# A spiking delta-rule attention block with routed experts: the first right-hand side formed ahead of the decay step, a later decay step put behind the first tile

## The reference, cut to what matters

```python
mem = DECAY * mem + sdt
hard = (mem > THR)                      # spike
mem = mem - spike * THR
alpha = sigmoid(abt + alpha_spike * spike)
beta  = sigmoid(bbt + sum(spike * beta_spike))
alpha = where(any hard, alpha, 1); beta = beta * any hard
s = s * alpha
u = einsum(kt, s)
s = s - beta * outer(kt, u) + beta * outer(kt, vt)
out = einsum(s, qt)
```

## Time and profile before

| | |
|---|---|
| three runs, us | 2068.42, 2074.34, 2077.52 (median 2074.34) |
| profiled execution, us (its span; the page shows nothing around it) | 2078.1 |
| mean granted TensorE clock in it | 0.858 |
| busy: TensorE, VectorE, ScalarE, GpSimd | 70%, 62%, 29%, 17% |
| chunks 0 to 6, end of the solve | 224.2, 428.5, 647.6, 865.3, 1076.7, 1288.8, 1503.7 |
| chunks 0 to 6, start of w0 | 230.7, 440.1, 657.5, 875.1, 1085.1, 1300.3, 1513.5 |
| chunks 0 to 6, start of w1 | 239.5, 448.9, 666.2, 883.9, 1093.9, 1309.1, 1522.2 |

### The profile page before, as it was taken

The page is one execution under the profiler, slowest core; times in us unless marked ns, Lnnn a source line. Parts: engine busy times, 40 slices in busy tenths (PEclk is TensorE's granted clock), DMA queues, the critical chain, the costliest instruction groups (busy, mean ns, idle before and its releaser), DMA issues. The chain is left out here.

```text
span 2078.1 us, 46460 instructions
## 1 busy us (share of the span) xinstructions
PE 1457.7 (70%) x18280; PEld 903.1 (43%) x18280; DVE 1279.4 (62%) x3385; ACT 596.6 (29%) x1212; POOL 348.5 (17%) x505
## 2 busy tenths in 40 slices
PE   1246886788778877797779776977797779566551
PEld 0113463256334643464336433653365336345541
DVE  1737766865577647865786478557965675343335
ACT  1132124322521243123413341324223412212221
POOL 2120031003200140014101410140013101100005
PEclk9577998899779988999799879987998789769995
DMA  2161000000010001000100010001000100302112
GB/s 72 72 253 22 19 10 7 21 19 21 2 26 19 10 13 27 16 12 13 27 16 12 12 27 16 12 13 27 11 17 12 23 16 12 103 17 76 33 30 81
DMA packets 110570, 64.74 MB, mean 31 GB/s; under 512 B 79873, under 2 KB 91329, under 8 KB 110354
## 3 DMA queue, kind: packets, MB, share of 16 engines
q1 hardware_dynamic: 99186, 38.52, 7.1%
q10 hardware_dynamic: 8448, 16.78, 2.2%
q0 software_dynamic: 2720, 6.36, 1.0%
HBM read 27.39 MB, written 34.24 MB: 30 GB/s over the span
## 5 line engine op out<-in xcount | busy, mean ns | idle before, releaser
L775 POOL COPY kx<-kend_t 32x256 f32<-32x256 f32 x256 | 113.1, 442 | 859.6 <-PE ps L1274 843.3
L1655 DVE SCALAR_TENSOR_TENSOR state<-state,gam,ps 128x128 f32<-128x128 f32 x512 | 137.5, 341 | 74.3 <-PE ps L1274 74.3
L1211 PE MATMUL ps<-wv,ident 128*128 128x512 f32 x320 | 169.1, 661 | 9.2 <-DVEq L1590 9.2
L1607 DVE TENSOR_TENSOR nv<-ps,nrm 128x512 f32<-128x512 f32 x64 | 44.2, 691 | 182.1 <-PE ps L1146 181.6
L1467 DVE TENSOR_TENSOR kq_leaf<-kq,eleaf 128x1024 f32<-128x1024 f32 x32 | 39.7, 1239 | 161.4 <-ACT dleaf L892 114.5
L1274 PE MATMUL ps<-w,kx 128*64 128x128 f32 x2048 | 132.5, 285 | 0.0
L1579 DVE TENSOR_TENSOR tmp<-kq,kq_blk 128x31 f32<-128x31 f32 (+15 forms) x248 | 115.2, 464 | 12.7 <-ACT mem L827 6.7
L1274 PEld LDWEIGHTS ps<-w,kx 128*64 128x64 f32 x2048 | 116.9, 143 | 13.6 <-issue 13.6
L1069 PE MATMUL ps<-yt,headind 128*16 128x512 f32 x128 | 87.1, 819 | 38.6 <-ACT yt L865 28.6
L1211 PEld LDWEIGHTS ps<-wv,ident 128*128 128x128 f32 x320 | 64.9, 213 | 90.4 <-issue 74.5
L1107 PE MATMUL ps<-kq_pair 64*32 64x32 f32 x2048 | 60.3, 220 | 61.5 <-DVE ab L1514 56.5
(11 more groups left out here) (317 smaller groups left out, 3188.3 us busy)
## 6 DMA issues: line engine op xcount, KB each, us to landing
slot_d<-zeros ACTq DMA_DIRECT2D x16, 1024.0 KB, 13.1
a_d<-kq_pair SPq DMA_DIRECT2D x8, 512.0 KB, 2.6
kq_blk<-a_d SPq DMA_DIRECT2D x32, 128.0 KB, 3.6
u_d<-kq SPq DMA_DIRECT2D x8, 512.0 KB, 2.6
ub<-u_d SPq DMA_DIRECT2D x128, 32.0 KB, 2.0
wall<-in_w SPq DMA_DIRECT2D x8, 512.0 KB, 8.0
xin<-slot_d SPq DMA_DIRECT2D x39, 64.0 KB, 1.8
made_d<-ye SPq DMA_DIRECT2D x39, 64.0 KB, 1.5
```

Source lines behind the costliest of these rows:

```text
L775: m = pool.tensor_copy(kx[part, :, b4, :], kend_t[part, g, 2 * q:2 * q + 2, :])
L1211: pe.matmul(bw.t[:, :], ident[:, :], wv[:, 0:512], start=True, stop=True)
L1655: k = dve.scalar_tensor_tensor(out=state[:, hp, b, :], in0=state[:, hp, b, :], scalar=gam[:, hp, b:b + 1], in1=bd[j].t[:, DV * x:DV * x + ...
```

## The change

VectorE's instructions are put in another order: `aff` and step 0 stand behind r0 and ahead of nv1, no longer ahead of r0. TensorE's step 1 (ab2 alone) stands at the end of tile 0, behind d0, no longer between v1 and w0. TensorE's other steps, and all of ScalarE's, GpSimd's and SyncE's instructions, stay where they are.

```diff
@@ TensorE, body @@
                     if i + 1 < TILES:
                         values(c, i + 1)
-                    if nxt and i + 1 < STEPS:
+                    if nxt and 0 < i < STEPS - 1:
                         decays(nxt, i + 1)
...
                         if b4 >= 2:
                             m.then_inc(bd[b4 % 2].full.sem, 1)
+                    if nxt and i == 0:
+                        decays(nxt, 1)
@@ VectorE, body @@
             solve(c, nxt, last)
             values(c, 0)
-            if last:
-                head_on_vector(dve, last, room, "aff")
-            if nxt:
-                decays(nxt, 0)
             for i in range(TILES + 1):
...
                     dve.tensor_tensor(r[:, :, :], nv[:, :, :], bp.t[:, :].rearrange("p (h v) -> p h v", v=DV),
                                       ALU.subtract).then_inc(bp.drained.sem, 1)
+                    if i == 0:
+                        if last:
+                            head_on_vector(dve, last, room, "aff")
+                        if nxt:
+                            decays(nxt, 0)
                     if i + 1 < TILES:
                         values(c, i + 1)
```

## The result

The changed kernel takes 2084.8 us (median of 20 runs), the kernel before 2072.1 us (20 runs beside them): ratio 1.0063, 95% interval 1.0041 to 1.0086, that is +13 us (+8.5 to +17.8). A later series on another chip gave 1.0065 (1.0028 to 1.0103). The forecast was 2081 and +6.6 us: right in direction and inside its range, too small by half, and on the other side of the 0.5% that the text had set as no change.

A forecast was written before the change was run, and what follows sets the result against it. No engine fills the span; a chain of handovers bounds the kernel. 11.2 us lost behind d0 less 4.6 gained in front gives +6.6 us, added to the 2074.34 median: 2081 us, 0.3% slower, range 2066 to 2091.

The forecast's parts named there:

- ab2 behind d0: Tile 1: r1 hangs on alpha2, which needs ab2, so w1 starts 1.6 us later; 11.2 us over seven chunks.
- w2: After w1: 1.3 us of slack is left before w2, so nothing more is late.
- r0 in the front: Before w0: r0 delays ab1, v1, w0 by 0.61 us in five chunks, 3.05 us; hidden in chunks 1 and 5.
- The low clock: Chunks 3 and 6: w0 moves into the 1.2 GHz stretch, taking back 0.6 us each, 1.2 us.
- the gain: Solve to w0 over seven chunks: 8.86 from ab2 leaving, less 3.05 for r0 and 1.2 for the clock, 4.6 us.
- The rival's: Before ab1: longer TensorE idling makes the clock fall more often, 1.34 us per low stretch; 2088 us, slower; chance 0.24.
- three signs of being wrong: w0 ahead of ab1; w0 to w1 below 9.7 us; or 1.2 GHz stretches in fronts that had none.
- w0 released by r0: Front: early r0 lets w0 start once `ub` has landed, as in chunk 7; 2064 us, faster; chance 0.08.
- The covered wait: Behind d0: r1 comes in time and r0 costs nothing, ab2 only changes place; 2071.5 us, no change; chance 0.10.

The follow-up runs named there:

- the filler: The changed kernel plus one filler product (two passes of 512 columns) on TensorE between ab0 and ab1; 1.0062 of the kernel before.
- TensorE's half alone: The kernel before with only the change's TensorE hunks, ab2 behind d0, VectorE's order as before; 1.0092 of the kernel before, +19 us.
- the second one: Profile of the unaltered changed kernel run once more beside two others on one chip; 1.0065 of the kernel before, profiled execution 2076.4 us.
- e5_spread: Against the changed kernel: only ab0 in front, ab1 and cnt0 behind p1, ab2 behind y0, r1 ahead of alpha1; 1.0114 of the kernel before, +24 us.
- v1 first: The changed kernel with ab2 behind p1 and v1 moved on TensorE between ab0 and ab1; 0.9939 and 0.9992 of the kernel before in two series.
- e2_vector_only: The kernel before with only the change's VectorE hunks, TensorE as before; 1.0006 of the kernel before, +1 us.

## Why the prediction was right, and where it fell short

- **ab2 behind d0** (forecast w1 1.6 us later, 7 x 1.6 = 11.2): right. At full clock w0 to w1 is 10.36 against 8.77, and with the filler, which keeps the clock up from w0 to w1, the seven chunks give 11.2 us. r1 behind alpha2 ends the wait, as forecast, and moving ab2 ahead in tile 0 takes 0.6 us of it away in each chunk; the other 1.0 is ab2's own room. The forecast had cnt1 ahead of r1's end and costing nothing; so it is, but by 0.36 us only, and r1 ahead of alpha2 gives back no more than that.
- **w2** (forecast "nothing more is late"): nearly. w1 to w2 is 7.90 against 7.82, 0.6 us over seven chunks.
- **r0 in the front** (0.61 us in five chunks, hidden in two): right by mechanism. In chunk 4 of the changed kernel alpha0 waits 2.51 us and r0 is free; with TensorE's half alone, w0 waits for r0. That r0 had to move for ab2's move to be worth anything was only half seen: the 0.24 us between r0 and w0 was in the rows.
- **The low clock** is the term that was mis-sized. I let it take 0.6 us in two chunks. In the changed kernel's profiles every front whose ab1 waits 1.6 us or more has a low stretch behind it that reaches w0 or ends just at it: four of seven, and six of seven in the second one. The other profiles bear this out. In the thirteen that have ab1 in front (all but e5_spread's), the granted clock fell between the start of that wait and w0 in 30 of the 31 fronts where ab1 waited 1.6 us or more, in 5 of the 6 where it waited 1.20 to 1.45 us, and in none of the 54 where it waited 1.12 us or less. The one of the 31 that kept its clock is chunk 0 of before (1.78 us). From w0 to w1 the low clock takes 75.36 - 72.41 = 2.95 us (2.0 in the second), and up to w0 the gain was 3.03 us, not 4.6 (3.65 in the second). Together with w2: 11.19 + 0.56 + 2.95 - 3.03 = 11.7, against the forecast 6.6 and the measured 13. So the forecast's mechanism carried the sign. The rival's, to which I gave 0.24 and the time 2088, carried 2.95 of the 5.1 us that were missing in this stretch, and the shorter gain up to w0 another 1.6. Of the prediction's three signs of being wrong one came true: chunks 0 and 4, at full clock from the solve to w1 before, have a low stretch in both profiles.

  By kind of front, from the solve to w1: where the clock is low ahead of ab0, 20.3 us became 20.7 (+0.4; forecast 1.6 - 1.15); where it is low behind ab1, 18.55 became 19.9 (+1.3; forecast 1.6 - 0.5); at full clock 17.2 became 18.2, seen only with the filler. None of the 14 fronts in the changed kernel's two profiles is at full clock from the solve to w1, as chunk 4 was before; that shift of kinds is part of the 11.7. It also makes the 3.03 us up to w0 partly luck: chunk 1 gained 2.57 us (forecast 1.15), as its fillers now ran at full clock, and chunks 4 and 6 lost 1.91 and 0.51 (forecast gains of 0.54 and 0.5), as theirs did not. The prediction had counted chunks 3 and 6 alone as low; in the same trace chunk 2 was low behind ab1 as well (0.50 from 653.4 to 656.7), and chunks 1 and 5 ahead of ab0.

  The Trainium skill (TensorE: Matmul & The Clock Gate, section "A second HAM failure mode: psum-queue depth-cycling") has short idle times between groups as a cause of such swings. These fronts agree; w6, which follows an idle time of 1.7 us at full clock in both profiles of the changed kernel as in the earlier trace rows, does not. But that row, which the prediction set against its rival, is no rule: in six of the 98 tiles 6 in chunks 0 to 6 of the fourteen profiles the clock did fall at w6 (last section).
- **w0 released by r0** fell as forecast: ab1 and cnt0 still stand ahead of w0. **The covered wait** fell too: w1's row names r1.

## What to carry to other kernels

When a product is moved later to free a front, follow the order of the engine that reads it: everything behind that read in the engine's queue moves with it, here the next tile's right-hand side, and so does what the read sets free, here the bank that cnt1 needs. A handover that runs 5 us early is no slack once another engine's instruction ahead of it in the queue waits. And price a longer idle time on TensorE by what runs next: a clock that falls as a tile of small products starts is dearer (6 to 8 us for one tile) than one that falls ahead of it (1.3).

## What the runs showed of the hardware

When the clock falls as a tile starts, it can stay low through nearly the whole tile, although TensorE is busy. In chunk 4 of the spread kernel w0 still started at full clock; the granted clock fell 0.15 us later, and from 1091 to 1108 it was 0.51 on average, with TensorE busy for 16.34 of the 17.00 us. Tile 0 took 18.5 and 18.8 us in two chunks there and 15.7 to 16.3 in three with v1 first, where full clock gives 11.1 and 9.7. So a start at full clock does not keep a tile from it.

The same happens in tiles that no kernel here changed. In chunk 7 the clock fell 0.7 to 2.0 us behind w0's start in the five profiles where tile 0 took 12.1 to 12.3 us instead of 7.7. In six of the 98 tiles 6 it fell 0.3 to 0.5 us behind w6's start, and w6 to w7 took 15.8 to 17.6 us, 11.3 to 13.1 in all but one of the others. TensorE in chunk 4 of e2_vector_only, w6 and what follows, then a stretch of that tile:

```profile
1155.86 1.59 PE L1232 MATMUL ps<-r,ub 128*128 128x128 f32 x8 [1.68 <-DVE r L1641]
1157.38 2.25 PE L1134 MATMUL ps<-state,kq_start 64*32 64x128 f32 x32
...
1156.40:1166.40 10.00, 9.74 (x128) 7.11 (x128) 5.67 (x19) 2.19 (x5) 0.00 (x0) 0.50 0.02 4
```

Each such tile makes an execution 4 to 6 us longer, which is a part of why single executions of one kernel differ. Why the clock does not recover in these, and does in chunk 0 of the changed kernel, where it fell 0.6 us ahead of w0 and was back within p1, the rows do not tell.
